# An own order on every engine for the last two attention steps of a gated cross-attention kernel, with the last value products in two halves of queries

## The reference

```
q = layernorm(x) @ Wq      -> [B, 512, H=16, D=128]
k = ctx @ Wk ; v = ctx @ Wv -> [B, 512, 16, 128]
q, k = rmsnorm(q, gq), rmsnorm(k, gk)
attn = softmax(q k^T / sqrt(128))
x = x + tanh(g) * ((attn v) merged over heads) @ Wo
```

## Time and profile before

| | |
|---|---|
| time, median of 3 runs | 1491.29 us (1490.92 to 1491.99) |
| the profiled execution | 1491.8 us |
| its span, first to last instruction | 1490.0 us |
| PE busy | 1442.1 us, 97% |
| DVE, ACT, POOL busy | 74%, 66%, 58% |
| PE matmuls | 8058 |
| mean granted clock of PE | 0.992 |
| chain that ended last | PE 85%, DVE 5%, POOL 5%, issue 2%, ACT 2% |

### The profile page before, as it was taken

How to read it: one execution, slowest core, us unless ns; L and a number is a source line. 1 busy time by engine, 2 the same in 40 slices (tenths; PEclk the granted TensorE clock), 3 DMA queues, 4 the chain that set the end, 5 groups by cost and what they waited for, 6 DMA issues and landing times.

```text
span 1490.0 us, 23928 instructions
## 1 busy us (share of the span) xinstructions
PE 1442.1 (97%) x8058; PEld 1227.7 (82%) x8058; DVE 1107.0 (74%) x2098; ACT 977.1 (66%) x2223; POOL 861.2 (58%) x702
## 2 busy tenths in 40 slices
PE   7899899999999999999999999999999999999997
PEld 5678788888887888888888888888888887878885
DVE  7877777777777777777777777777777776787776
ACT  6865466666766667676676767667676675666563
POOL 4775355555554466666675757566576754654431
PEclk9999899999999999999999999999999999999999
DMA  8410011111111333334343433443434331321002
GB/s 318 155 65 1 29 44 43 43 49 45 43 56 45 117 116 134 131 129 150 104 142 128 136 131 115 136 139 115 137 118 144 115 123 33 103 71 36 8 1 85
DMA packets 55497, 142.76 MB, mean 96 GB/s; under 512 B 5393, under 2 KB 5393, under 8 KB 55377
## 3 DMA queue, kind: packets, MB, share of 16 engines
q1 hardware_dynamic: 51616, 128.90, 25.2%
q0 software_dynamic: 3760, 12.32, 2.9%
HBM read 126.79 MB, written 14.42 MB: 95 GB/s over the span
## 4 chain that ended last, share of the span: by engine, by line
PE 85%; DVE 5%; POOL 5%; issue 2%; ACT 2%; DMA 0%; POOLq 0%; SPq 0%; ACTq 0%; DVEq 0%
PE j_bank L471 11%; PE j_bank L473 11%; PE j_bank L472 11%; PE w_bank L471 10%; PE w_bank L473 9%; PE w_bank L472 9%; PE t_bank L525 7%; PE s_bank L471 4%; PE s_bank L473 4%; PE s_bank L472 4%; PE t_bank L492 2%; PE t_bank L590 1%; PE t_bank L591 1%; PE w_bank L621 1%; POOL xnT_raw L1589 1%
## 5 line engine op out<-in xcount | busy, mean ns | idle before, releaser
L806 ACT ACTIVATE prob<-s_bank,neg_bias,q_scale 128x512 f32<-128x512 f32 x256 | 198.5, 776 | 206.7 <-DVE neg_bias L1233 206.7
L1076 DVE TENSOR_TENSOR probT_lo<-t_bank,probT_hi 128x512 fp32r<-128x512 f32 x264 | 179.1, 689 | 181.4 <-ACT probT_hi L767 181.3
L1282 DVE SCALAR_TENSOR_TENSOR x_sb<-w_bank,inv_sum,x_sb 128x512 f32<-128x512 f32 x256 | 190.0, 743 | 0.9 <-PE w_bank L473 0.9
L1212 DVE TENSOR_REDUCE neg_max<-s_bank 128x1 f32<-128x512 f32 x256 | 169.2, 682 | 0.0
L1529 POOL TENSOR_TENSOR xnT_lo<-xnT_raw,xnT_hi 128x512 fp32r<-128x512 f32 (+2 forms) x47 | 126.3, 2689 | 60.6 <-ACT xnT_hi L767 60.6
L525 PE MATMUL t_bank<-ident,prob 128*128 128x128 f32 x1024 | 154.2, 273 | 7.0 <-ACT prob L806 4.9
L1569 POOL TENSOR_TENSOR q_scale<-q_ss,minus_half 128x4 f32<-128x4 f32 x64 | 65.8, 1028 | 155.1 <-DVE q_ss L1225 155.1
L767 ACT CAST probT_hi<-t_bank 128x512 fp32r<-128x512 f32 x264 | 152.1, 589 | 3.8 <-PE t_bank L483 2.1
L471 PE MATMUL j_bank<-wkv_lo,cT_hi 128*128 128x256 f32 x512 | 145.9, 285 | 3.2 <-DVE oT_lo L1076 3.2
L525 PEld LDWEIGHTS t_bank<-ident,prob 128*128 128x128 f32 x1024 | 122.9, 140 | 28.0 <-ACT prob L806 6.4
L473 PE MATMUL j_bank<-wkv_hi,cT_lo 128*128 128x256 f32 x512 | 145.6, 284 | 0.0
(11 more groups left out here) (266 smaller groups left out, 4437.7 us busy)
## 6 DMA issues: line engine op xcount, KB each, us to landing
stage<-w SPq DMA_DIRECT2D x96, 256.0 KB, 2.9
xnT_raw<-w_gu SPq DMA_DIRECT2D x31, 704.0 KB, 4.1
cT_raw<-w_gu SPq DMA_DIRECT2D x31, 704.0 KB, 4.6
xnT_raw<-w_dn SPq DMA_DIRECT2D x16, 768.0 KB, 4.3
cT_raw<-w_dn SPq DMA_DIRECT2D x15, 768.0 KB, 4.8
planes<-bits SPq DMA_DIRECT2D x16, 512.0 KB, 4.2
y<-stage SPq DMA_DIRECT2D x31, 256.0 KB, 3.9
x_sb<-x SPq DMA_DIRECT2D x5, 1024.0 KB, 8.3
```

Source lines behind the costliest of these rows:

```text
L806: nc.scalar.activation(prob[:, i, :], s_bank[i % 2][:], ACT.Exp, bias=neg_bias[:, u % 2, i:i + 1], scale=q_scale[:, u % 2, i:i + 1], accum ...
L1076: return nc.vector.tensor_tensor(dst, src, hi, ALU.subtract)
L1212: nc.vector.tensor_reduce(neg_max[:, u % 2, i:i + 1], s_bank[i % 2][:], AX_X, ALU.max, negate=True).then_inc(own_max, 1)
L1282: nc.vector.scalar_tensor_tensor(out=here, in0=w_bank[0 if packed else i % 2][:], scalar=inv_sum[:, w % 2, i:i + 1], in1=here, op0=ALU.mul ...
```

## The change

Steps 64 (`LAST_SCORES`) and 65 (`LAST_VALUES`) get lists of their own on PE, ACT and DVE. What is computed stays the same.

- Step 64, PE: query_squares is called after scores(0), not after scores(1). scores(2) is called before values, in j_bank[1]. probs(0) to probs(3) go to four different banks and no longer wait for p_lo. project_out(0) to (3) are spread between probs(1), probs(2) and probs(3).
- Step 64, ACT: softmax 0 and 1 are called before values_hi, and each probs_hi takes turns with the next softmax.
- Step 64, DVE: inverses comes ahead of the maxima, maximum(2) and shift(2) ahead of add_before(3) and values_lo. add(3) of item 62 is no longer put off, it ends step 64.
- Step 65: the value product is done in two halves of 256 queries (`last_values`), each into 256 columns of a bank of its own; the first half needs only probs_lo 0 and 1. Both hi casts and both lo subtractions are halves too. The four output products go to four banks (w_bank, s_bank), so that none waits for an add.
- Step 63: the lo part of item 63's squares is subtracted by DVE (`last_squares_lo`, between key_lo and probs_lo(3)), no longer by POOL.

```
+LAST_SCORES = NI
+LAST_VALUES = NI + 1
-    return not (T0 <= t <= T0 + NB) and t not in (LAST[0] + 2, T0 - 1, NI + 1)
+    return not (T0 <= t <= T0 + NB) and t not in (LAST[0] + 2, T0 - 1, LAST_SCORES, LAST_VALUES)
+        def score_bank(t, i):
+            return (s_bank[0], s_bank[1], j_bank[1], s_bank[0])[i] if t == LAST_SCORES else s_bank[i % 2]
+        def prob_bank(t, i):
+            return (t_bank[1], t_bank[0], s_bank[1], j_bank[1])[i] if t == LAST_SCORES else t_bank[P_BANK[i]]
+        def value_bank(half):
+            return (j_bank[0], t_bank[0])[half][:, 0:S // 2]
+        def out_bank(t, i):
+            return (w_bank + s_bank)[i] if t == LAST_VALUES else w_bank[i % 2]
...
-                    need(pe, p_exp, 4, u, i - 1)
+                    need(pe, p_exp, 4, u, (0, 0, 0, 1)[i] if t == LAST_SCORES else i - 1)
...
-                    else:
+                    elif t != LAST_SCORES:
                         need(pe, p_lo, 4, u, (0, None, 1, 3)[i])
...
+                def last_values(half):
+                    here = slice(half * S // 2, (half + 1) * S // 2)
+                    need(pe, p_lo, 4, w, 2 + 2 * half)
+                    need(pe, v_lo, 1, w, 1)
+                    for j in range(NT):
+                        last = product(value_bank(half), [a[:, w % 2, 1, j * P:(j + 1) * P] for a in kv],
+                                       [a[:, j, here] for a in probT], j == 0, j == NT - 1)
+                    last.then_inc(pv_mm, 1)
...
+                    if t == LAST_VALUES and i == 2:
+                        need(pe, o_lo, 1, w, 2)
...
+                    if t == LAST_VALUES:
+                        need(pe, w_added, 4, w, 0)
+                    else:
+                        need(pe, w_added, 4, w, i if packed else i - 1)
...
+                if t == LAST_SCORES:
+                    scores(0)
+                    query_squares()
+                    scores(1)
+                    scores(2)
+                    values()
+                    probs(0)
+                    scores(3)
+                    probs(1)
+                    project_out(0)
+                    project_out(1)
+                    probs(2)
+                    project_out(2)
+                    probs(3)
+                    project_out(3)
+                    return
+                if t == LAST_VALUES:
+                    last_values(0)
+                    last_values(1)
+                    for i in range(NT):
+                        project_out(i)
+                    return
...
+                def last_values_hi(half):
+                    need(act, pv_mm, 1, w, 1 + half)
+                    need(act, w_mm, 4, w - 1, 4)
+                    copy_hi(oT[0][:, half * S // 2:(half + 1) * S // 2], value_bank(half)).then_inc(o_hi, 1)
...
+                if t == LAST_SCORES:
+                    softmax(0)
+                    softmax(1)
+                    values_hi()
+                    probs_hi(0)
+                    softmax(2)
+                    probs_hi(1)
+                    softmax(3)
+                    probs_hi(2)
+                    probs_hi(3)
+                    return
...
+                if t == LAST_SCORES:
+                    squares_out()
+                    inverses()
+                    maximum(0)
+                    maximum(1)
+                    shift(0)
+                    shift(1)
+                    maximum(2)
+                    shift(2)
+                    add_before(3)
+                    values_lo()
+                    maximum(3)
+                    shift(3)
+                    probs_lo(0)
+                    add(0)
+                    probs_lo(1)
+                    add(1)
+                    probs_lo(2)
+                    probs_lo(3)
+                    add(2)
+                    add(3)
+                    return
+                if t == LAST_VALUES:
+                    inverses()
+                    last_values_lo(0)
+                    last_values_lo(1)
+                    for i in range(NT):
+                        add(i)
+                    return
...
+                    if t == NI - 1:
+                        last_squares_lo()
                     probs_lo(3)
...
-                squares_lo()
+                if t != NI - 1:
+                    squares_lo()
```

More of the change, by code:

```diff
@@ L510, in scores @@
                         need(pe, kT_lo, 1, u, 1)
-                    need(pe, p_exp, 4, u, i - 1)
-                    product(s_bank[i % 2][:], [a[:, u % 2, i * P:(i + 1) * P] for a in qT],
+                    need(pe, p_exp, 4, u, (0, 0, 0, 1)[i] if t == LAST_SCORES else i - 1)
+                    product(score_bank(t, i)[:], [a[:, u % 2, i * P:(i + 1) * P] for a in qT],
                             [a[:, u % 2, 0, :] for a in kv]).then_inc(s_mm, 1)
@@ L521, in probs @@
                         need(pe, q_ss_out, 1, u, 1)
-                    else:
+                    elif t != LAST_SCORES:
                         need(pe, p_lo, 4, u, (0, None, 1, 3)[i])
                     for j in range(4):
-                        last = pe.transpose(t_bank[P_BANK[i]][:, j * P:(j + 1) * P], prob[:, i, j * P:(j + 1) * P],
+                        last = pe.transpose(prob_bank(t, i)[:, j * P:(j + 1) * P], prob[:, i, j * P:(j + 1) * P],
                                             ident[:])
@@ L548, in project_out @@
                         wait(pe, y_copied, min(b, NB))
-                    need(pe, w_added, 4, w, i if packed else i - 1)
-                    product(w_bank[0 if packed else i % 2][:], [a[:, i * P:(i + 1) * P] for a in oT],
+                    if t == LAST_VALUES:
+                        need(pe, w_added, 4, w, 0)
+                    else:
+                        need(pe, w_added, 4, w, i if packed else i - 1)
+                    product(w_bank[0][:] if packed else out_bank(t, i)[:], [a[:, i * P:(i + 1) * P] for a in oT],
                             [a[:] for a in wo]).then_inc(w_mm, 1)
@@ L805, in softmax @@
                     need(act, p_turned, 4, u - 1, i + 1)
-                    nc.scalar.activation(prob[:, i, :], s_bank[i % 2][:], ACT.Exp,
+                    nc.scalar.activation(prob[:, i, :], score_bank(t, i)[:], ACT.Exp,
                                          bias=neg_bias[:, u % 2, i:i + 1], scale=q_scale[:, u % 2, i:i + 1],
@@ L814, in probs_hi @@
                     copy_hi(probT[0][:, :, i * P:(i + 1) * P],
-                            t_bank[P_BANK[i]][:].rearrange("p (j q) -> p j q", j=4)).then_inc(p_hi, 1)
+                            prob_bank(t, i)[:].rearrange("p (j q) -> p j q", j=4)).then_inc(p_hi, 1)
                 def values_hi():
@@ L937, in step @@
                     return key_parts, key_query_parts, query_squares
+                if t == LAST_SCORES:
[10 more added lines that the diff above has]
+                if t == LAST_VALUES:
+                    last_values_hi(0)
+                    last_values_hi(1)
+                    return
                 if fresh(t):
@@ L1211, in maximum @@
                     need(dve, s_mm, 4, u, i + 1)
-                    nc.vector.tensor_reduce(neg_max[:, u % 2, i:i + 1], s_bank[i % 2][:], AX_X, ALU.max,
+                    nc.vector.tensor_reduce(neg_max[:, u % 2, i:i + 1], score_bank(t, i)[:], AX_X, ALU.max,
                                             negate=True).then_inc(own_max, 1)
@@ L1248, in values_lo, with last_values_lo @@
                     lower(oT[1][:], j_bank[0][:], f32(oT[0][:])).then_inc(o_lo, 1)
+                def last_values_lo(half):
+                    here = slice(half * S // 2, (half + 1) * S // 2)
+                    need(dve, o_hi, 1, w, 1 + half)
+                    lower(oT[1][:, here], value_bank(half), f32(oT[0][:, here])).then_inc(o_lo, 1)
                 def probs_lo(i):
@@ L1254, in probs_lo @@
                     hi, lo = [a[:, :, i * P:(i + 1) * P] for a in probT]
-                    lower(lo, t_bank[P_BANK[i]][:].rearrange("p (j q) -> p j q", j=4), f32(hi)).then_inc(p_lo, 1)
+                    lower(lo, prob_bank(t, i)[:].rearrange("p (j q) -> p j q", j=4), f32(hi)).then_inc(p_lo, 1)
                 def values_rows():
@@ L1282, in add_of @@
                     nc.vector.scalar_tensor_tensor(
-                        out=here, in0=w_bank[0 if packed else i % 2][:], scalar=inv_sum[:, w % 2, i:i + 1],
+                        out=here, in0=w_bank[0][:] if packed else out_bank(t, i)[:], scalar=inv_sum[:, w % 2, i:i + 1],
                         in1=here, op0=ALU.mult, op1=ALU.add).then_inc(w_added, 1)
@@ L1354, in take, with last_squares_lo @@
                                                    in1=here, op0=ALU.mult, op1=ALU.add).then_inc(y_added, 1)
+                def last_squares_lo():
+                    need(dve, q_squared, 2, t, 2)
+                    lower(sqs[1][:], squares(t), f32(sqs[0][:])).then_inc(sq_lo, 1)
+                if t == LAST_SCORES:
[20 more added lines that the diff above has]
```

(5 more changed lines are left out.)

## The result

The changed kernel takes 1482.9 us (median of 5 runs, 1479.61 to 1483.39). The kernel before has 1491.09 in the same comparison (5 runs, 1490.06 to 1491.99). The ratio is 0.9943, 95% interval 0.9932 to 0.9953. Another 5 runs of the same changed kernel, on another occasion, have a median of 1483.95 beside 1490.84, ratio 0.9951 (0.9938 to 0.9965). So it's faster by 0.5 to 0.6%. The forecast was 1484.1, its range began at 1482.8.

The account below looks back on a forecast made before the run. PE, busy 97% of the span, bounds the kernel, so only idle time, slow matmuls and the tail at the end can be won: -6.76 - 0.4 = -7.2 us, giving 1484.1 us, range 1482.8 to 1487.2.

Parts of the forecast that it names:

- the tail: From the last add to the span's end, 3.70 us before: 0.4 us off, bounds nothing and 0.8.
- Squares and inverses: Before step 64's first shift: squares on DVE win 0.28 us, inverses ahead of the maxima cost 0.35, shift 0.07 later.
- The lists of step 64: PE, ACT and DVE order in step 64: half products begin 12.02 us after its start, not 15.95; 3.93 won.
- The clock: PE's granted clock stays at 1.00 to 1478; about 1.5 of the 6.76 us won in steps 64 and 65.
- Step 65: Half value products and outputs without a pause; 6.76 us won to the last add, 3.93 of them in step 64.
- The clock's fall: Rival, chance 0.12: the clock still falls once around last_values and project_out, costing 1.5 us, giving 1485.6.
- a slower ring: Rival, chance 0.12: step 64's chain of waits through project_out(2), add(0) and probs(3) loses 1.8 us, giving 1485.9.
- a bound of DVE's pace: Rival, chance 0.04: something such as DVE's pace, about 11 us, holds step 64; only step 65 gains, giving 1488.1.

Follow-up runs that it names:

- steps 63 and 64 only: Changed kernel with step 65 as before (whole values, two output banks); ratio 0.9966 to the kernel before, 23.82 us from step 64's start to the span's end.
- step 65 only: Kernel before with only step 65's lists, halves and banks, item 62's last add ending step 64; ratio 0.9977, 25.97 us from step 64's start to the span's end.
- last values whole: Changed kernel with the last value product whole but four output banks; one run, 23.46 us from step 64's start to the span's end.
- old banks: Changed kernel with turned probabilities in their old banks with the old waits, order still new; one run, 22.52 us from step 64's start to the span's end.

## Why the prediction was right, and where not

What the forecast said of steps 64 and 65 held. The step that failed is the tail: it took 0.4 us off, with 0.8 as the most, and 0.95 came off. Beside it the forecast put at nothing what differs between executions of the same code.

Times from step 64's start (less 1460.83 in the forecast, less 1456.47 in the profile after):

| point | forecast | measured |
|---|---|---|
| squares_out | 1.87 | 1.87 |
| first shift | 4.75 | 4.72 |
| first exp | 5.00 | 4.97 |
| project_out(0) | 7.89 | 7.85 |
| probs(3) | 10.77 | 10.75 |
| first half product | 12.02 | 12.01 |
| end of the last add | 18.71 | 18.58 |
| end of the span | 22.0 | 21.33 |

- **Squares and inverses.** Both terms were right, 0.28 won and 0.35 spent. The experiments give 0.33 for either.
- **The lists of step 64.** Right to 0.02 us at the half products. The lists and banks were worth 3.9 us, of which the banks hold 1.2. Some 0.45 of the 3.9 is the clock, though, and no merit of the lists: that much step 64 lost of its 15.95 us when only the pause was filled.
- **The clock.** It stayed up, as forecast, and filling the old pause prices that at 1.3 us where I had 1.5. The rule of the Trainium skill (TensorE: Matmul & The Clock Gate, Part 4: PE-mode transpose), that transposes don't count as a busy PE in the way matmuls do, made no difference here: with four sets of them in the step the clock fell only with the long pause, and it read 1.00 with the pause filled.
- **Step 65.** Forecast 6.69 from the first half to the end of the last add, measured 6.57. I had put the last four adds 0.71 apart; from 1472.29 to 1473.62 two of them take 1.33.
- **The tail.** This is the step that failed. The prediction held that the large store "is out at 1478.5, before three of the tiles", so that the last tile lands as one alone does, in 2.7 to 3.0 us, and took 0.4 off. The tail went from 3.70 to 2.75, 0.95 off, beyond even the bound of 0.8. It is the larger part of the 0.65 us by which the stretch was better. Both halves of the step were wrong. A last tile that nothing holds up lands in 2.0 to 2.1 us, and the span then ends 2.5 after the last add (steps 63 and 64 only, step 65 only, last values whole). And in the changed kernel the large store isn't out of the way: store and tiles still run as one train, and the span ends 7.3 us after the store's issue, as before. The prediction's own rows had this: 1474.9 + (1490.0 - 1482.67) = 1482.2 for the end of the span, where it wrote 1482.8, and 21.4 for the stretch, where 21.33 was measured. The forecast would have been 1483.5.
- **The range.** Its ends don't follow from the bounds that it names: they give 1484.1 - 0.4 - 0.3 = 1483.4 to 1484.1 + 0.4 + 0.8 + 0.3 = 1485.6, where the prediction has 1483.0 to 1485.3, and nothing is named for the 1482.8. Nor is there a term for what differs between executions. The start of step 64 varies by 5 us between executions of unchanged code, and whole runs of the changed kernel by 1.2 (the second five runs) to 3.8 us (the first five). The stretch implies 1491.09 - 7.8 = 1483.3 for the first five and 1490.84 - 7.8 = 1483.0 for the second. The first median, 1482.9, lay 0.4 on the fast side, the second, 1483.95, 0.9 on the slow one. The lower end, 1482.8, left no room for that beside the tail. On which side of it a median fell was chance: the two medians of the same kernel are 1.05 us apart.
- **The rivals.** The clock's fall, a slower ring and a bound of DVE's pace didn't come. In the ring the wait for add(0) is there as described; with probs(3) called ahead of it, and without the one for add(1), 0.36 is won (20.68 against 21.04).

What stays open: why the granted clock is low for about 20 us of the first 200 in one execution and for 9 in another. It was seen, not varied. Open too is how long a pause the clock stands here: in the last two steps no run had a pause between 1.40 and 2.04 us. And most variants have a single profile.

## What to carry to other kernels

At the end of a software pipeline the lists made for full steps leave pauses that nothing fills. Lay the last steps out by hand from the start-to-start times of the timeline (0.60 us, not the 0.69 that a lone operation shows); here that gave each point up to the last add to 0.15 us. Look for what a pause costs behind it: 2 us of idle PE cost another 1.3 us in slow matmuls. Count the end of a kernel with stores on one queue from the issue of the train's first store as well as from the last add, and take the later of the two. When two versions differ by less than the runs do, count from the first instruction that the change can touch.

## What the runs showed of the hardware

- Seven matmuls that nobody reads made the end of a kernel 1.3 us faster, by keeping the granted clock at 1.00. It fell after pauses of 2.04 us (the kernel before, step 65 only). It didn't after one of 0.98 (old banks), nor after those of 1.40 ahead of the outputs (steps 63 and 64 only, last values whole).
- A store of 1 MB and four of 256 KB behind it on one queue moved nearly without a break (375 GB/s over three us of it in the changed kernel), and the span ended 7.3 us after the first was issued (nine profiles). With the large store 5.7 us or more ahead of the last add, the span ended 2.5 us after that add.
- A 256 KB store lands in 2.0 to 2.1 us with the large store out of the way, in 2.3 to 2.5 in the changed kernel, in 3.0 to 3.8 in the kernel before, and in 3.6 to 4.6 with the large store issued just ahead of it.
- The granted clock in the first 200 us differs between executions of one kernel (0.93 or 0.97 from 50 to 100 us), and step 64 of it began at 1461.15 or at 1456.47.
